# Fetching projection weight slices from ScalarE's DMA queue instead of SyncE's, in a fused retention and FP4 linear layer

## What is computed

```python
x = L0_attn_x
xn = _layernorm(x, axis=-1)
x = x + _L0_attn_ref(xn, ...) + _L0_ffn_ref(xn, ...)
# _L0_attn_ref: 16 heads of 64
q, k, v = heads((x @ Wq + bq) * scaling), heads(x @ Wk + bk), heads(x @ Wv + bv)
ret = einsum('bhid,bhjd->bhij', q, k) * D          # causal decay per head
ret = ret / clip(abs(ret.sum(-1)), 1.0)
g = groupnorm(einsum('bhij,bhjd->bhid', ret, v)) * gn_w + gn_b
attn_out = silu(x @ Wg + bg) * g @ Wo + bo
# _L0_ffn_ref: x and weight rounded to FP4 values with one scale per 16
out = einsum('mbk,nbk->mn', xdq, wdq) * output_scale + bias
```

## Time and profile before

| | |
|---|---|
| three runs | 2421.79, 2427.49, 2429.26 us (median 2427.49) |
| profiled execution, own time | 2426.53 us |
| its span | 2424.7 us, 40980 instructions |
| busy | PE 2191.4 us (90%), DVE 1550.5 (64%), POOL 646.0 (27%), ACT 557.0 (23%) |
| DMA | 270.66 MB, mean 112 GB/s |
| slice fetches (wring<-parts) | 256 of 512.0 KB, median 3.2 us from issue to landing |

### The profile page before, as it was taken

How to read it: one execution, slowest core, us unless ns; L and a number is a source line. 1 busy time by engine, 2 the same in 40 slices (tenths; PEclk the granted TensorE clock), 3 DMA queues, 4 the chain that set the end, 5 groups by cost and what they waited for, 6 DMA issues and landing times.

```text
span 2424.7 us, 40980 instructions
## 1 busy us (share of the span) xinstructions
PE 2191.4 (90%) x12972; PEld 1159.5 (48%) x13024; DVE 1550.5 (64%) x3798; ACT 557.0 (23%) x811; POOL 646.0 (27%) x460
## 2 busy tenths in 40 slices
PE   1278887879789999999999999999999999999999
PEld 1144443444345555555545555555555555555543
DVE  7766677788775656666655656666655666666642
ACT  5523231112112222222222222222222222222210
POOL 1022331312223233233223233233223223223221
PEclk9689998889889999999999999999999999999999
DMA  7964234234332233333222233333223233333322
GB/s 282 363 187 133 79 112 123 65 99 121 92 95 89 84 108 108 100 100 99 95 87 91 79 108 108 100 100 99 96 87 99 80 98 108 100 100 99 99 74 112
DMA packets 189250, 270.66 MB, mean 112 GB/s; under 512 B 118272, under 2 KB 139264, under 8 KB 188160
## 3 DMA queue, kind: packets, MB, share of 16 engines
q1 hardware_dynamic: 189184, 269.83, 34.9%
HBM read 202.68 MB, written 37.75 MB: 99 GB/s over the span
## 4 chain that ended last, share of the span: by engine, by line
PE 65%; DVE 20%; issue 5%; ACT 3%; DMA 3%; SPq 2%; POOL 1%; DVEq 0%; POOLq 0%; ACTq 0%
PE mm L1101 42%; PE mm L1065 7%; PE four L1154 5%; PE mm L1077 2%; PE four L1149 2%; PE tp L1111 2%; PE four L1121 2%; PE tp L1133 1%; SPq L268 1%; DMA xt<-in_x 1%; PE tp L1163 1%; DVE xa L725 1%; DVE xa L726 1%; DVE attn L945 1%; DVE gs L943 1%
## 5 line engine op out<-in xcount | busy, mean ns | idle before, releaser
L1101 PE MATMUL mm<-xnT,wring 128*128 128x512 f16 x6144 | 1390.4, 385 | 57.4 <-DMA wring<-parts 25.3
L1101 PEld LDWEIGHTS mm<-xnT,wring 128*128 128x128 f16 x6144 | 603.3, 99 | 772.6 <-issue 76.0
L1065 PE MATMUL mm<-wo,yT 128*128 128x512 f16 x1536 | 348.6, 384 | 0.0
L426 POOL TENSOR_TENSOR qparts<-qT,qparts 128x512 f16<-128x512 f32 x64 | 81.3, 1270 | 670.5 <-ACT qT L580 670.5
L1065 PEld LDWEIGHTS mm<-wo,yT 128*128 x1536 | 150.3, 100 | 174.8 <-issue 8.5
L444 POOL TENSOR_TENSOR yT<-attn,gate 128x512 f32 x64 | 82.2, 1285 | 536.5 <-ACT attn L614 509.7
L943 DVE TENSOR_REDUCE gs<-attn 128x8 f32<-128x512 f32 x64 | 43.9, 686 | 226.5 <-ACT attn L600 226.5
L911 DVE TENSOR_TENSOR probs<-four,dmask 128x512 f32<-128x512 f32 x128 | 82.3, 684 | 139.2 <-PE four L1121 137.5
L426 POOL TENSOR_TENSOR kparts<-kT,kparts 128x512 f16<-128x512 f32 x64 | 76.1, 1189 | 324.2 <-ACT kT L580 309.1
L688 DVE BATCH_NORM_STATS2 ls<-xt 128x6 f32<-128x512 f32 x64 | 41.2, 685 | 171.7 <-DMA xt<-in_x 171.2
L600 ACT ACTIVATE attn<-four 128x260 f32<-128x260 f32 x128 | 42.6, 384 | 389.3 <-PE four L1154 378.0
(11 more groups left out here) (165 smaller groups left out, 2466.8 us busy)
## 6 DMA issues: line engine op xcount, KB each, us to landing
wring<-parts SPq DMA_DIRECT2D x256, 512.0 KB, 3.2
xt<-in_x SPq DMA_DIRECT2D x33, 512.0 KB, 3.5
out<-res SPq DMA_DIRECT2D x32, 512.0 KB, 2.8
res<-in_x SPq DMA_DIRECT2D x28, 512.0 KB, 4.2
parts<-xqT SPq DMA_DIRECT2D x36, 256.0 KB, 4.8
parts<-xnT SPq DMA_DIRECT2D x36, 256.0 KB, 3.4
res<-in_w_f SPq DMA_DIRECT2D x16, 512.0 KB, 3.9
yT<-in_w_k SPq DMA_DIRECT2D x1, 4096.0 KB, 15.2
```

The source lines that it names most:

```text
L426: nc.gpsimd.tensor_tensor(parts[:, 1], full[:], parts[:, 0], ALU.subtract)\
L1065: last = MM(mm[0][:], y[:, yj, k, ds(q * P, P)], wo[:, wj, k, h * GROUP:(h + 1) * GROUP], start=(n == 0), stop=(n == 3 * KT - 1))
L1101: last = MM(mm[n % 2][:], wring[:, n, wj, k, :], xnT[:, parity, xj, k, :], start=(j == 0), stop=(j == 3 * KT - 1))
```

## The change

The function `load_slices` and all its calls go from SyncE's program. In ScalarE's `evacuate`, right behind the last ACTIVATE of a projection's evacuation, the fetch into the slot of that projection is issued from ScalarE's queue. In FIRST_A, for u = 0, two waits stand ahead of it until the split weights are stored in DRAM; on SyncE they stood ahead of the fetches in the first body.

```diff
-                def load_slices(u, which=range(4)):
-
-                    for n in which:
-                        w(f"mm{n % 2}_full", mm_use(phase, u, n))
-                        sp.dma_start(wring[:, n].rearrange("p a b c -> p (a b c)"),
-                                     a["parts"][n, ds(q * 2 + 1 + u, 1)].rearrange("a p n -> p (a n)"))\
-                          .then_inc(s["w_" + MATS[n]], 16)
-
...
                 if (phase, i) == (FIRST_A, 0):
 
                     load_x()
-                    for h in range(2):
-                        sp.wait_ge(stored[h], 16 * 2 * (PAIRS + 1))
-                    load_slices(0, range(2))
                     store_parts(3)
-                    for h in range(2):
-                        sp.wait_ge(stored[h], 16 * 4 * (PAIRS + 1))
...
                     load_res(f_rows[0])
-                    load_slices(0, (2,) if (phase, i) == (FIRST_A, 0) else range(3))
...
                     move_x_parts()
-                    load_slices(0, (3,))
-                    load_slices(1)
                     move_x()
...
                     load_res(f_rows[0])
-                    load_slices(0, (0,))
                     move_xq(1, wf[:, :, ds(q * (2 * P), P)])
                     load_res(f_rows[1])
-                    load_slices(0, (1, 2, 3))
                     move_x_parts()
-                    load_slices(1, (0, 1))
                     move_x()
-                    load_slices(1, (2, 3))
                     move_xq(3, wf[:, :, ds(q * (2 * P) + P, P)])
...
                     load_res(a["x"][rows, :])
-                    load_slices(0)
                     move_x_parts()
-                    load_slices(1)
...
                     nc.scalar.activation(dst, mm[n % 2][:], ACT.Silu if n == 3 else ACT.Identity,
                                          bias=bias[:, n, pair(u)], scale=down[MATS[n]])\
                       .then_inc(s[f"mm{n % 2}_free"], 1)
+                    if phase == FIRST_A and u == 0:
+                        for h in range(2):
+                            act.wait_ge(stored[h], 16 * (2 if n < 2 else 4) * (PAIRS + 1))
+                    act.dma_start(wring[:, n].rearrange("p a b c -> p (a b c)"),
+                                  a["parts"][n, ds(q * 2 + 1 + u, 1)].rearrange("a p n -> p (a n)"))\
+                       .then_inc(s["w_" + MATS[n]], 16)
```

## The result

The changed kernel takes 2432.23 us (median of 20 runs, 2426.84 to 2439.80) against 2426.30 for the kernel before (20 runs beside them, 2421.79 to 2435.23): a ratio of 1.0024, with a 95% interval of 1.0014 to 1.0035. That is 5.9 us more, less than the 0.3% (7.3 us) that the prediction took as the least that one measurement can tell from no change; the 20 runs on each side resolve it. The forecast was 2431.0, in a range of 2420 to 2440. The profiled execution took 2432.73 us, its span is 2430.9; against the one before (2426.53) it is 6.2 us longer.

A forecast was written before the change was run, and what follows sets the result against it. TensorE is busy 90% of the span, but SECOND goes by VectorE's chain and MIDDLE can only lose. The terms 5.2 - 1.8 + 1.0 = +4.4 us on 2426.53 gave 2431 us, range 2420 to 2440.

The forecast's parts named there:

- SECOND, what is removed: In all four SECOND bodies the 4.8 us wait ahead of project(1,v) goes; one of 5.5 us appears behind it.
- SECOND, what the moved wait costs: In SECOND `attend(0)` restarts at half clock and delays VectorE's group norm: +5.2 us over four bodies.
- FIRST, the gain: Second body of FIRST_B: the load of xt leaves SyncE's queue earlier: -1.8 us, bounds 0 and -3.2.
- this bound, that VectorE may lose what it wins: The 0 end of the gain in FIRST_B: GpSimd's gate products run just there.
- FIRST, the loss: End of FIRST_A: the fetch of g on ScalarE stands behind the evacuation, 2.1 us later: +1.0 us, bounds 0 and 3.
- the sign of 2.2 to 3.5 us: In FIRST, TensorE's waits for slices of 1.3 to 1.5 us would become 2.2 to 3.5 us.
- The first body of FIRST_A, and MIDDLE: ScalarE's wait for stored weights, and its eight fetch issues of 0.33 us per MIDDLE body, cost nothing.
- The first: Rival: waits for slices are on the path; all 25.3 us go (2401 us), or half (2414 us); chance 0.10.
- The second: Rival: ScalarE's queue delays the copy of `attend` in 24 MIDDLE bodies, up to 2451 us; chance 0.07.
- The third, a costlier clock: Rival: restarts in FIRST and slow followers of `attend(0)` in SECOND also cost: +12.3 us, 2439 us; chance 0.15.
- the fourth: Rival: the clock holds or the moved wait in SECOND costs nothing: -3.4 us, 2423 us; chance 0.18.

The follow-up runs named there:

- experiment 1: Kernel before, all fetches still on SyncE, but in SECOND v, q and g of the first pair issued ahead of the transpose of xq: 2435.43 us, ratio 1.0040.
- experiment 5: Changed kernel plus 40 unused 128x252 matmuls ahead of `attend(0)` in each body of SECOND: 2408.45 us against 2426.20 for the kernel before, ratio 0.9929.
- experiment 4: Changed kernel with slice v of the first pair in SECOND issued by SyncE again, ahead of the load of res: 2422.35 us, ratio 0.9972 to kernel before.
- experiment 10: Changed kernel with a wait ahead of each fetch on ScalarE's queue until the evacuation's last ACTIVATE is finished: 2439.26 us, ratio 1.0062 to the kernel before.
- experiment 7: Changed kernel plus 40 unused matmuls once between SECOND and MIDDLE: 2424.73 us against 2427.11 for the kernel before, ratio 0.9982.
- experiment 9: Kernel before, fetches on SyncE, plus 76 unused matmuls ahead of `attend(1)` in SECOND and GpSimd's bias addition moved in MIDDLE: 2393.11 us, ratio 0.9862.
- experiment 6: Changed kernel with GpSimd's bias addition in MIDDLE moved behind decay_q(1): 2418.11 us against 2427.11 for the kernel before, ratio 0.9947.
- experiment 8: Changed kernel plus 40 unused matmuls ahead of `attend(0)` and 76 ahead of `attend(1)` in SECOND, bias addition moved in MIDDLE: 2402.64 us, ratio 0.9883.

## Why the prediction was right, step by step

- **SECOND, what is removed: right.** No wait for a slice is left there, project(1,v) follows the state increments, and the new wait is 5.6 us in three bodies (forecast 5.5) and 4.8 in the first.
- **SECOND, what the moved wait costs: right, the reason tested from both sides.** Forecast +5.2, measured +5.7. By its own formula the four delays of the group norm were 0.94, 1.95, 1.44 and 0.83 (5.2 in sum) and came as 0.99, 1.19, 1.49 and 0.88 (4.6). The second was too large, as the clock came back in the middle of `attend(0)`: its second part took 2.72, not 3.5 us. The 1.1 us beyond that is a balance that the prediction did not have: 2.6 us by which VectorE's own operations became longer, less 1.5 us elsewhere. That the sum comes within 0.5 us of the forecast is in part luck, the more so as SECOND alone moved by 2.7 us between kernels that share its program. Experiments 1 and 5 make and remove the loss without touching the queue, and experiment 4 takes it away with a wait.
- **FIRST, the gain (-1.8): it came, and was given back.** The load of xt goes out at 288.83 instead of 311.58, VectorE starts on it at 311.33 instead of 316.04, and `attend(0)` starts 1.83 us earlier with no wait for `carry` (first row below, against the earlier trace rows). Part of that only made up for a slow clock: 48 matmuls from 308.86 on took 12.22 us, and 10.53 before. TensorE, then ScalarE, second body of FIRST_B, after:

```profile
338.83 0.83 PE L1133 MATMUL four<-state,qT 128*128 128x130 f32 x6
...
350.12 1.12 PE L1147 MATMUL tp<-ident,work 128*128 128x128 f32 x4 [2.67 <-DVE kn L887]
```

```profile
340.55 2.00 ACT L534 ACTIVATE wo<-yT,cols  x1
342.44 0.66 ACT L584 ACTIVATE attn<-four 128x260 f32<-128x260 f32 x2
```

  Then ScalarE's 2 us instruction for the output weights stands ahead of its copy of `attend(0)`, which now has to wait for it, and 11 us later TensorE waits 2.67 us for `kn` (1.67 before) and restarts slowly (its transposes take 1.12 instead of 0.66 us, and the projection behind them starts at 353.53, where the kernel before has 353.23). No run tested that the one causes the other. The prediction named this bound, that VectorE may lose what it wins, and took the wrong end of it. FIRST as a whole was +1.4 where -0.8 was forecast; this is the term that was mis-sized, by about 2 us.
- **FIRST, the loss (+1.0): wrong in its premise.** "On ScalarE it stands behind the evacuation" does not hold for the issue of a DMA. It ran mostly 0.13 to 0.19 us into an ACTIVATE, or beside the table load, so the four waits for slices stayed at 1.15, 1.35, 1.15 and 1.26 us (before 1.30, 1.36, 1.43 and 1.48), and the sign of 2.2 to 3.5 us there did not come. Experiment 10 shows that the wait would otherwise have been about as worked out at the end of FIRST_A (3.3 us where 3.5 was said), but that the slow restart would not have come on top: it moves from one projection to the next, and both TensorE and VectorE begin the next body no later than in the kernel after. That the forecast of 2431.0 lies only 1.2 us under the measured 2432.2 is in part luck: FIRST came out 2.2 us above its -0.8, and the stretch ahead of it, which had no term, 1.1 us under nothing.
- **The first body of FIRST_A, and MIDDLE (0): right.** The eight issues of a body take 0.34 us each (SyncE: 0.33), and MIDDLE and TAIL together differ by 0.2 us. The steadiness hides something that the prediction did not see: bodies that a shift elsewhere makes 5.7 us longer or shorter. Here both kernels fell on the same side of it. Experiments 5 and 7 fell on the other, and a small loss would then have looked like a large gain.
- **The rivals.** The first is out by experiments 1, 4 and 9. The second is out, at 0.34 us an issue. The third, a costlier clock, did not come: experiment 10 brings its restarts in FIRST (the projections take 7.0 to 8.2 instead of 5.4 us), and they do not fall on the path. Of the fourth, the clock did not hold in this kernel. Experiment 5 makes it hold, and SECOND then ends 2.1 us earlier than before, which agrees with the rival's term of -2.6 as far as single executions can show. Experiment 4 takes 2422.35 us, close to the 2423 that were worked out, but by another way: there the wait stands ahead of the projection again. The chances hold a slip: the forecast and the fourth rival have 0.68 together, so "0.66 with a little of the third" does not add up; nothing else hangs on it.

## What to carry to other kernels

A wait of the busiest engine that is followed by a longer one on the same engine is not a gain to be had. Before it is removed, ask which matmuls will stand right behind the next wait. They pay for the slow restart, and it is better paid by work with slack than by work that another engine's chain hangs on. And compare a change of some microseconds body by body: stages that it does not touch may move by three times its effect.

## What the runs showed of the hardware that was not expected

- **A DMA issued from ScalarE's queue does not wait for the ACTIVATE written ahead of it.** It mostly starts 0.13 to 0.19 us after the evacuation's first ACTIVATE, which takes 0.78 us, and in the rows above 0.27 us after the start of a table load, 1.03 us before that table load's own ACTIVATE; behind a wait for the ACTIVATE's semaphore it goes out 0.24 us after its end. So a DMA that overwrites what an ACTIVATE ahead of it still reads would need that wait; here only the matmuls read the slot. The Trainium skill (PSUM — Partial Sum Buffer, Engine vs sequencer instructions) keeps instructions of the datapath and those of the sequencer apart as two classes; the rows of experiment 10 agree, and show the DMA's issue on the sequencer's side.
- **VectorE's copy of 64x65 elements took 2.48 us beside GpSimd's 2.35 us addition, and 0.39 to 0.41 us without it.** It ends 0.26 us after GpSimd does, as if it had stood still. The Trainium skill (SBUF — State Buffer, SBUF: two separate sides) says that GpSimd and a VectorE operation in one of its two-port modes, or with two inputs in SBUF, share one pair of ports: whichever starts first holds it for the whole instruction, and the other blocks. No row shows the copy's mode, but the trace agrees: GpSimd started 0.13 us earlier. Experiment 6 removes the meeting by order alone.
- **The clock at a restart.** After 5.6 us of standing, the 24 matmuls of `attend(0)` took 5.4 us in two of three bodies; behind extra matmuls and 0.2 to 2.5 us of standing they took 2.9. Waits of 2.0 to 2.4 us in MIDDLE were followed by half clock within 2 us of the restart, while waits of 2.22 and 2.54 us behind extra matmuls in SECOND (experiments 5 and 8) were not: their stretches stay at 1.00. So the length of the one wait did not decide it here. Extra matmuls in the waits of SECOND, 76 or 116 in a body, cost nothing that the time shows, and the bodies were 1.5 to 2.9 us shorter than before.
